# A Fourier-operator tower on one core: fused stage in a new order of units, spectra stored by group, mode and image, mix product and its copy in halves

## The chip, the cores and the metric

The kernel runs on one NeuronCore of a Trainium2 chip. The metric is the device time of one execution in microseconds. The engines are TensorE (PE, with its weight loads PEld), VectorE (DVE), ScalarE (ACT), GpSimd (POOL) and SyncE (SP, whose queue issues most DMAs). Everything is fp32.

## The reference, cut to what matters

Nearly all of the work that the change touches is the tower of four Fourier layers. 64 images of 64 by 64 pixels with 3 channels are lifted to 64 channels, and then:

```python
h = jnp.einsum('bhwi,ic->bhwc', x, fc0_w) + fc0_b          # the lift
for l in range(LAYERS):                                     # 4 layers
    xf = jnp.fft.rfft2(h)
    top = jnp.einsum('bixy,ioxy->boxy', xf[:, :, :M1, :M2], w1)     # 16 x 16 modes
    bot = jnp.einsum('bixy,ioxy->boxy', xf[:, :, -M1:, :M2], w2)
    sc = irfft2(top and bot in place, zero elsewhere)
    y = sc + einsum('bihw,oi->bohw', h, pw_w[l]) + pw_b[l]
    y = (y - mean(y)) * rsqrt(var(y) + EPS) * gamma[l] + beta[l]    # over images and pixels
    h = gelu(y)
h = gelu(h @ fc1_w + fc1_b) @ fc2_w + fc2_b
```

An attention block, two mixtures of experts and a second attention follow on the small result; the change does not touch them.

## The kernel before, in words

The program is a chain of stages. Between two stages every engine waits for all the others (`phase_end`).

1. **spectrum0** makes the spectra of the lifted input. PE transforms the 3-channel input and turns it into 64 channels in 16 rounds (`channels0`); in each round DVE and ACT copy four PSUM banks into one of three buffers `spec0`. After every fourth round SP stores a 4 MB buffer to `spec_in` in DRAM. POOL meanwhile prepares 1 MB of weights in four pieces (`gpsimd_even`), each piece loaded, computed and stored. SP's queue has `wait_ge(even_stored, 64)` and the load of those weights ahead of the four stores; round 12 waits until the first store has landed.
2. **mix** (four times, one per layer). The modes come in 8 chunks, each of 2 units (NU = 16 units). For a chunk SP loads 2 MB of spectra (`s_sb`, three buffers) and 2 MB of mode weights (`w_sb`), ACT and DVE each turn one half over to the other partitions (`rotate`), and for each unit PE runs `product` (the pointwise weights on the spectra, into four banks), ACT copies the four banks to `x2` (`copy_product`), and PE runs `spectra` (64 matmuls of 64 by 64 weights with 128 columns, one pair of weight halves per mode) into the same banks. Then ACT squares the result twice with a running sum (`square`), DVE multiplies it with `x2` twice (`cross`) and transposes it (`turn`), and SP stores it to `spec_out`. Unit n uses banks 0 to 3 or 4 to 7 by turns. In `s_sb` an element is found at (image, mode), so one mode of all images lies 64 elements apart. The sums give the mean and the variance of the next normalisation. Near the end (`ahead`) SP waits until chunk 6 has landed, then loads what the next stage starts with.
3. **fused stage** (layers 0, 1 and 2). It works on 32 pairs of images. For pair p and quarter T of its pixels: `rows_of` (half of the inverse transform, DVE turns it over), `y_of` (the other half, `spectral`, plus in layer 0 the pointwise product of the input), in layers 1 and 2 DVE adds the stored pointwise part (`add`), ACT applies Gelu in place (`gelu`), DVE transposes it (`px_turn`), PE makes the next layer's pointwise part (`next_of`), ACT copies it out (`evict`) and squares the PSUM slot with a running sum, and PE transforms the transposed pixels forward (`w_dft`, `h_dft`, DVE turning each over with `w_turn` and `h_turn` into `xs`). SP stores the pointwise part of a pair to `y_dram` (two DMAs of 1 MB) and loads the pair after next (2 MB in layers 1 and 2; 48 KB pieces of the input in layer 0), and stores four pairs' spectra at once.
4. **last stage** (layer 3's inverse, the two dense layers), then the small tail.

The fused stage's order is written out by hand: each engine has a loop over n with calls for pair n (`now`), n - 1 (`before`) and n + 1 (`after`). PSUM is cut into slots of two banks; slots 0 and 1 serve `rows_of`, `y_of` and `next_of`, banks 4 to 7 the forward transforms. A unit waits until the unit that used its slot before has been read out:

```python
ROWS_SLOT = (0, 1)
Y_SLOT = (0, 0, 1, 0)
NEXT_SLOT = (0, 1, 1, 1)
```

In layer 0 a `y` is read out by `gelu` (the semaphore `drained` is `h_made`), in layers 1 and 2 by `add` (`drained` is `y_added`). A slot of `next_of` is free when both the copy and the square have read it (`squared`).

## Time and profile before

| | before |
|---|---|
| runs (3) | 5169.06, 5176.79, 5186.94 us; median 5176.79 |
| the profiled execution | 5171.28 us, of which the span from first to last instruction 5169.4 us |
| PE, PEld busy | 3833.6 us (74%), 2200.9 us (43%) |
| DVE, ACT, POOL busy | 2339.6 us (45%), 2245.7 us (43%), 173.6 us (3%) |
| mean granted TensorE clock | 0.850 |
| moved by DMA | 800.11 MB, 155 GB/s on average |

No engine is busy all the time, and the stages have different limits, so the shares over the span say little; the stages are read one by one. The clock is a share: 1.0 is 2.4 GHz and 0.5 is 1.2 GHz, so 0.81 is a mixture in time of the two.

### The profile page before, as it was taken

The numbers are of one execution on the slowest core, as the hardware profiler recorded it, in microseconds if no ns is written. First come the engines' busy times: TensorE is split into PE (matmuls) and PEld (weight loads), VectorE is DVE, ScalarE is ACT, GpSimd is POOL, SyncE is SP. The second block draws the span as 40 slices with busy tenths as digits, with TensorE's granted clock in tenths as the row PEclk, the third lists the DMA queues.
The fourth block names the chain that finished last, engine by engine and source line by source line (L and its number), as shares of the span: only waits on it lengthen the run. The fifth ranks groups of instructions, "written<-read, shape, count | busy, mean of one in ns | idle before, by whom it ended". The sixth has DMA issues, their size and how long they took to land. (4 is left out here: it accounts for less than half of the span.)

```text
span 5169.4 us, 141776 instructions
## 1 busy us (share of the span) xinstructions
PE 3833.6 (74%) x64580; PEld 2200.9 (43%) x64580; DVE 2339.6 (45%) x2458; ACT 2245.7 (43%) x2564; POOL 173.6 (3%) x249
## 2 busy tenths in 40 slices
PE   5768878886856666765866667665769999676877
PEld 3544444444633333432643333333544444263342
DVE  2434434443445554553445555454433333355456
ACT  1434544443434444443444444443436666422222
POOL 1003100000000000000000000000000001200000
PEclk8889999997878888886878888888879999867878
DMA  6646544546556666655656656656654333101123
GB/s 232 250 138 166 142 124 124 140 123 211 193 174 184 177 172 193 182 170 183 231 159 179 189 176 175 190 165 200 238 192 155 143 145 130 36 1 43 25 65 76
DMA packets 162307, 800.11 MB, mean 155 GB/s; under 512 B 26889, under 2 KB 33361, under 8 KB 111854
## 3 DMA queue, kind: packets, MB, share of 16 engines
q1 hardware_dynamic: 150876, 776.16, 49.5%
q0 software_dynamic: 7936, 13.65, 0.8%
q8 instruction: 517, 8.47, 0.7%
q10 hardware_dynamic: 2898, 1.17, 0.1%
q14 instruction: 80, 0.66, 0.0%
HBM read 448.68 MB, written 342.23 MB: 153 GB/s over the span
## 5 line engine op out<-in xcount | busy, mean ns | idle before, releaser
L826 DVE TENSOR_TENSOR arena<-bank,arena 128x1024 f32<-128x1024 f32 x384 | 468.2, 1219 | 1047.0 <-PE bank L809 1047.0
L809 PE MATMUL bank<-fb,arena 64*64 64x128 f32 x16384 | 685.9, 304 | 299.7 <-issue 134.6
L809 PEld LDWEIGHTS bank<-fb,arena 64*64 64x64 f32 x16384 | 570.4, 197 | 639.9 <-issue 584.3
L1006 ACT ACTIVATE arena<-arena,shift,scale 128x1024 f32<-128x1024 f32 x256 | 317.7, 1241 | 862.0 <-DVE arena L826 853.7
L933 PE MATMUL bank<-arena,wst 64*64 64x512 f32 x3072 | 496.0, 687 | 146.8 <-issue 146.8
L603 PE MATMUL bank<-arena 64*64 64x128 f32 x8192 | 461.6, 393 | 132.5 <-ACT arena L631 100.0
L818 DVE STREAM_TRANSPOSE arena<-bank 128x1024 f32<-128x1024 f32 x256 | 317.6, 1241 | 518.4 <-PE bank L799 518.4
L964 PE MATMUL bank<-arena,ghq 32*32 32x256 f32 x12288 | 381.9, 501 | 190.5 <-issue 110.7
L603 PEld LDWEIGHTS bank<-arena 64*64 64x64 f32 x8192 | 408.2, 173 | 212.8 <-issue 186.8
L1013 ACT ACTIVATE arena<-bank 128x1024 f32<-128x1024 f32 x384 | 392.2, 1021 | 199.2 <-DVE arena L1046 141.8
L1046 DVE STREAM_TRANSPOSE arena<-arena 128x1024 f32<-128x1024 f32 x384 | 462.8, 1212 | 0.6 <-ACT arena L1003 0.6
L799 PE MATMUL bank<-arena,ga 64*64 64x256 f32 x4096 | 321.0, 430 | 126.6 <-DMA arena<-spec_out 54.9
L964 PEld LDWEIGHTS bank<-arena,ghq 32*32 32x32 f32 x12288 | 223.2, 119 | 403.4 <-issue 357.4
L1014 ACT ACTIVATE bank<-bank 128x1024 f32<-128x1024 f32 x384 | 391.7, 1020 | 0.0
L947 PE MATMUL bank<-arena,fwq 32*32 32x256 f32 x12288 | 321.7, 412 | 57.1 <-issue 45.7
L684 DVE SCALAR_TENSOR_TENSOR arena<-bank,arena 128x1024 f32<-128x1024 f32 x128 | 156.3, 1225 | 411.6 <-ACT arena L642 410.9
L1003 ACT ACTIVATE arena<-bank,shift,scale 128x1024 f32<-128x1024 f32 x128 | 154.2, 1205 | 410.2 <-PE bank L913 410.2
L799 PEld LDWEIGHTS bank<-arena,ga 64*64 64x64 f32 x4096 | 176.0, 147 | 354.5 <-issue 286.5
L575 PE MATMUL bank<-arena,wst 64*64 64x512 f32 x512 | 232.8, 1033 | 84.8 <-ACT arena L626 84.8
L642 ACT ACTIVATE arena<-bank 128x1024 f32<-128x1024 f32 x128 | 131.2, 1025 | 363.6 <-PE bank L603 355.7
L1176 PE MATMUL bank<-arena,fc 64*128 64x512 f32 x1024 | 274.6, 635 | 18.9 <-ACT arena L1240 18.9
L1240 ACT ACTIVATE arena<-bank,fc1b 128x1024 f32<-128x1024 f32 x256 | 272.2, 1100 | 19.6 <-PE bank L1176 19.5
(240 smaller groups left out, 3961.5 us busy)
## 6 DMA issues: line engine op xcount, KB each, us to landing
y_dram<-arena SPq DMA_DIRECT2D x192, 1024.0 KB, 10.3
arena<-y_dram SPq DMA_DIRECT2D x96, 2048.0 KB
arena<-spec_in SPq DMA_DIRECT2D x32, 2048.0 KB, 7.9
spec_out<-arena SPq DMA_DIRECT2D x128, 512.0 KB, 8.7
arena<-in_w_modes SPq DMA_DIRECT2D x28, 2048.0 KB, 13.8
arena<-spec_out SPq DMA_DIRECT2D x112, 512.0 KB, 11.7
spec_in<-arena SPq DMA_DIRECT2D x24, 2048.0 KB, 7.6
spec_in<-arena SPq DMA_DIRECT2D x4, 4096.0 KB, 24.8
```

The costliest lines, as they stand in the source:

```text
L603: mm = pe.matmul(bank[4 * v + q][ROW[h], k * 2 * B:(k + 1) * 2 * B], w_sb[c % 3][ROW[row], mode, :], z[ROW[row], :, :, mode], start=(swap ...
L799: mm = pe.matmul(bank[2 * s + v][CHAN[par], :].rearrange("p (c r k) -> p r k c", c=16, r=2)[:, r], ga[k_p, r * S:(r + 1) * S], grp[p // Q ...
L809: mm = pe.matmul(hpx(bank[2 * s + i][CHAN[v], :])[:, :, j * S:(j + 1) * S], a2[p % 2][CHAN[i], :, v, 4 * T + j], hpx(fb2[CHAN[i], :]), sta ...
L818: dve.transpose(a2[p % 2].rearrange("p (v c) a m -> p v (c a m)", v=2)[:, :, hc * 512:(hc + 1) * 512], slot(s)).then_inc(rows_turned, 1)
L826: dve.tensor_tensor(chunk(p, T), slot(s), chunk(p, T), ALU.add).then_inc(y_added, 1)
L933: mm = pe.matmul(bank[2 * NEXT_SLOT[T] + v][CHAN[i], :], wst[CHAN[v], :], pb[p % NS][CHAN[v], i, T * BK:(T + 1) * BK], start=True, stop=Tr ...
L947: mm = pe.matmul(bank[4 + g][QUAD[c], 0:256], fwq[QUAD[g], s * 32:(s + 1) * 32], hT[p % 2][QUAD[g], i, :, s, c * CQ:(c + 1) * CQ], start=( ...
L964: mm = pe.matmul(bank[4 + c][QUAD[j], 256:512], ghq[QUAD[c], col:col + K1], t1[p % 2][QUAD[c], hh * 2 + v, :, :, ri * M2:(ri + 1) * M2], s ...
L1006: act.activation(chunk(p, T), chunk(p, T), ACT.Gelu, bias=shift[:], scale=scale[:]).then_inc(h_made, 1)
L1013: act.activation(chunk(p, T), slot(NEXT_SLOT[T]), ACT.Copy).then_inc(evicted, 1)
L1014: act.activation(slot(NEXT_SLOT[T]), slot(NEXT_SLOT[T]), ACT.Square, accum_out=acc[:, p * 4 + T:p * 4 + T + 1]).then_inc(squared, 1)
L1046: dve.transpose(hT[p % 2].rearrange("p i h s c -> p i (h s c)")[:, :, T * BK:(T + 1) * BK], chunk(p, T)).then_inc(px_turned, 1)
```

## The change

**spectrum0.** The stores of the four buffers no longer stand behind `even_stored`; the wait and the load of the even weights come after them. `spec_in` and `spec0` are laid out by (group of 8 images, mode, image of the group), and each copy of two banks is cut into two of one bank.

**mix.** `s_sb` and `r_sb` have the new layout, so that 8 images of a mode lie side by side and 4 modes of a group are 32 elements side by side. `product` is now 16 matmuls of 256 columns (before: 4 of 512 and 8 of 256), and it and its copy are in two halves, each with its own count: PE starts `spectra` on the first two banks when their copy is done. On ACT the order is square of the first half, both copies of the next unit, square of the second half; on DVE the cross of the second half comes first, before any square. `turn` waits for both squares.

**Fused stage.** A new order of the units on PE, ACT and DVE; `y_of(p, 1)` moves to slot 1; `h_dft` comes a pair later; `gelu` of quarter 3 moves behind the next pair's first units on ACT; the square reads what `evict` has written in SBUF (into a scratch buffer at the arena's end) and stands apart from it, so that a slot is free after the copy; SP's reload of a pair's buffer also waits for its squares.

**Elsewhere.** Some small tensors move into the arena, which grows by 1024 elements; scratch places shift; two more waits for `zeroed`. The last stage and the tail are as before.

The core of the diff:

```diff
 # spectrum0, SP's queue
-            sp.wait_ge(even_stored, 64)
-            load_even(sp, 0)
             for t in range(NB):
                 sp.wait_ge(fc0_first, 4 * t + 4)
                 sp.wait_ge(fc0_second, 4 * t + 4)
...
+                sp.dma_start(spec_in[:, :, gs].rearrange("h p g x -> p h (g x)"), spec0[t % 3]).then_inc(spec0_stored[min(t, 1)], 16)
+            sp.wait_ge(even_stored, 64)
+            load_even(sp, 0)
 # mix
-        s_sb = [at(S_AT + u * B * MC, B, MC) for u in range(3)]
+        s_sb = [at(S_AT + u * B * MC, NG, MC * GI) for u in range(3)]
...
-                        if q % 2 == 0:
-                            mm = pe.matmul(bank[4 * v + q][ROW[h], :], wst[ROW[0], :],
-                                           z[ROW[0], :, :, m0:m0 + 4].rearrange("p r b m -> p m r b"),
-                                           start=True, stop=True, tile_position=(0, h * C))
...
+                        for r in range(2):
+                            part = z[ROW[0], r] if q % 2 == 0 else z[ROW[1], 1 - r]
+                            w = wst[ROW[0], :] if q % 2 == 0 else (wst, wneg)[r][ROW[1], :]
+                            mm = pe.matmul(o[:, r], w, part[:, :, m0:m0 + 4, :].rearrange("p g m b -> p g (m b)"),
+                                           start=True, stop=True, tile_position=(q % 2 * C, h * C))
+                    if q % 2 == 1:
+                        mm.then_inc(prod_done, 1)
...
-                pe.wait_ge(prod_copied, l * NU + n + 1)
...
+                    if swap == 0:
+                        pe.wait_ge(prod_copied, (l * NU + n) * 2 + pair + 1)
...
-                                               w_sb[c % 3][ROW[row], mode, :], z[ROW[row], :, :, mode],
+                                               w_sb[c % 3][ROW[row], mode, :], z[ROW[row], :, :, mode, :],
 # fused stage
-        Y_SLOT = (0, 0, 1, 0)
+        Y_SLOT = (0, 1, 1, 0)
...
-            for n in range(NP + 1):
-                now, before, after = n < NP, n > 0, n + 1 < NP
+            for n in range(NP + 2):
+                now, before, after = n < NP, 0 < n <= NP, n + 1 < NP
                 if now:
                     y_of(n, 0)
-                if before:
-                    next_of(n - 1, 2)
-                if now:
                     y_of(n, 1)
+                if n > 1:
+                    h_dft(n - 2)
                 if before:
                     next_of(n - 1, 3)
...
-                act.activation(slot(NEXT_SLOT[T]), slot(NEXT_SLOT[T]), ACT.Square, accum_out=acc[:, p * 4 + T:p * 4 + T + 1]).then_inc(squared, 1)
+
+            def square(p, T):
...
+                act.activation(junk_p.rearrange("p (i x) -> p i x", i=2), chunk(p, T), ACT.Square,
+                               accum_out=acc[:, p * 4 + T:p * 4 + T + 1]).then_inc(squared, 1)
```

How the new order stands on the engines is best read from the programs' own rows. First PE in the fused stage of layers 1 and 2, from one `y_of(n, 0)` on. L809 is `y_of` (16 matmuls), L933 `next_of`, L799 `rows_of`, L947 `w_dft`, L964 `h_dft`; the ISA and REGISTER_ALU rows compute semaphore values. Before:

```order
L809 MATMUL bank<-fb,arena 64x2x64 x16
L922 REGISTER_ALU
L933 MATMUL bank<-arena,wst 64x512 x4
L903 REGISTER_ALU
L809 MATMUL bank<-fb,arena 64x2x64 x16
L922 REGISTER_ALU
L933 MATMUL bank<-arena,wst 64x512 x4
L890 ISA
L799 MATMUL bank<-arena,ga 64x16x16 x8
L947 MATMUL bank<-arena,fwq 32x256 x32
L809 MATMUL bank<-fb,arena 64x2x64 x16
```

The same place of the change, where L822 is `y_of`, L954 `next_of`, L812 `rows_of`, L970 `w_dft` and L985 `h_dft`:

```order
L822 MATMUL bank<-fb,arena 64x2x64 x32
L985 MATMUL bank<-arena,ghq 32x256 x64
L938 REGISTER_ALU
L948 REGISTER_ALU
L954 MATMUL bank<-arena,wst 64x512 x4
L903 ISA
L812 MATMUL bank<-arena,ga 64x16x16 x8
L822 MATMUL bank<-fb,arena 64x2x64 x16
L970 MATMUL bank<-arena,fwq 32x256 x32
```

The first two `y_of` now stand together, `h_dft` of an older pair fills the place after them, and one `next_of` has moved to the end of the turn.

ACT at the same stage. Before, L1006 is `gelu`, L1013 the copy and L1014 the square, always in this order:

```order
L1006 ACTIVATE arena<-arena,shift,scale 128x2x512
L1013 ACTIVATE arena<-bank 128x2x512
L1014 ACTIVATE bank,acc<-bank 128x1024
L1005 ISA
L1006 ACTIVATE arena<-arena,shift,scale 128x2x512
L1013 ACTIVATE arena<-bank 128x2x512
L1014 ACTIVATE bank,acc<-bank 128x1024
```

In the change L1027 is `gelu`, L1034 the copy and L1041 the square, which now reads the arena:

```order
L1034 ACTIVATE arena<-bank 128x2x512 x2
L1026 REGISTER_ALU
L1027 ACTIVATE arena<-arena,shift,scale 128x2x512
L1041 ACTIVATE arena,acc<-arena 128x1024
L1026 ISA
L1027 ACTIVATE arena<-arena,shift,scale 128x2x512
L1041 ACTIVATE arena,acc<-arena 128x1024
```

Two copies come first in a turn, and a square never stands between a copy and the next unit's use of its slot.

ACT in the mix, from the first copy of a product on. Before, L631 is the copy, L642 the square, L626 the turning over:

```order
L631 ACTIVATE arena<-bank 128x2048
L626 ACTIVATE arena<-arena 64x4096
L642 ACTIVATE arena,acc<-bank 128x1024 x2
L631 ACTIVATE arena<-bank 128x2048
L642 ACTIVATE arena,acc<-bank 128x1024 x2
```

In the change L634 is the copy, L646 the square, L628 the turning over:

```order
L646 ACTIVATE arena,acc<-bank 128x1024
L634 ACTIVATE arena<-bank 128x1024 x2
L646 ACTIVATE arena,acc<-bank 128x1024
L628 ACTIVATE arena<-arena 64x4096
L646 ACTIVATE arena,acc<-bank 128x1024
```

The copies of the next unit's two halves now stand between the two squares of this unit.

## Rows read from the trace of the kernel before

**Rows 1.** Windows: length, PE, PEld, DVE, ACT, POOL busy, clock, DMA share, GB/s

```profile
0.00:124.00 124.00, 68.61 (x460) 50.34 (x460) 34.03 (x42) 17.58 (x17) 25.30 (x37) 0.82 0.63 230
...
357.00:1217.00 860.00, 684.66 (x15360) 368.38 (x15360) 346.36 (x320) 405.31 (x513) 71.42 (x73) 0.93 0.53 139
1217.00:1451.00 234.00, 171.73 (x2434) 126.98 (x2434) 96.50 (x117) 97.46 (x92) 0.00 (x0) 0.81 0.62 216
1451.00:2431.00 980.00, 652.18 (x14336) 369.08 (x14336) 488.25 (x448) 422.48 (x513) 0.37 (x1) 0.81 0.59 174
...
2666.00:3622.00 956.00, 646.38 (x14336) 366.33 (x14336) 488.46 (x448) 422.50 (x513) 0.37 (x1) 0.82 0.62 180
```

**Rows 2.** Timeline of spectrum0, DVE and SP: start, us, what, idle before

```profile
93.26 2.35 DVE L341 COPY arena<-bank 128x1024 f32<-128x1024 f32 x2 [30.99 <-DMA spec_in<-arena]
...
77.25 22.74 SPq L245 DMA_DIRECT2D spec_in<-arena  x4
```

**Rows 3.** Timeline of PE, two units of the mix of layer 1

```profile
1286.24 7.21 PE L603 MATMUL bank<-arena 64*64 64x128 f32 x128 [2.06 <-ACT arena L631]
...
1299.00 7.17 PE L603 MATMUL bank<-arena 64*64 64x128 f32 x128 [2.09 <-ACT arena L631]
```

**Rows 4.** PE lines one by one: duration ns min/median/max

```profile
L575 PE MATMUL bank<-arena,wst x512: 1030/1032/1113, 135.9 to 3820.3; 64*64 64x512 f32 x171
...
L913 PE MATMUL bank<-arena,wx x1024: 586/589/1112, 367.3 to 1180.5; 64*64 64x512 f32 x171
...
L603 PE MATMUL bank<-arena x8192: 377/392/473, 141.6 to 3830.3; 64*64 64x128 f32 x200
...
L809 PE MATMUL bank<-fb,arena x16384: 266/275/479, 366.3 to 4473.6; 64*64 64x128 f32 x200
...
L799 PE MATMUL bank<-arena,ga x4096: 372/376/687, 361.2 to 4452.4; 64*64 64x256 f32 x196
```

**Rows 5.** Timeline of SP, end of the mix of layer 1

```profile
1414.85 4.88 SPq L523 DMA_DIRECT2D spec_out<-arena  x4
...
1451.88 0.82 SPq L769 DMA_DIRECT2D arena<-spec_out  x2
```

**Rows 6.** Timeline of PE, one pair of the fused stage of layer 1

```profile
2010.91 1.19 PE L809 MATMUL bank<-fb,arena 64*64 64x128 f32 x32
...
2013.55 1.19 PE L809 MATMUL bank<-fb,arena 64*64 64x128 f32 x32 [0.59 <-DVE arena L826]
2016.85 1.34 PE L933 MATMUL bank<-arena,wst 64*64 64x512 f32 x8 [2.11 <-issue]
...
2024.32 1.09 PE L799 MATMUL bank<-arena,ga 64*64 64x256 f32 x16 [0.57 <-DVE arena L826]
...
2028.80 1.19 PE L809 MATMUL bank<-fb,arena 64*64 64x128 f32 x32 [1.84 <-ACT bank L1014]
...
2032.57 1.32 PE L964 MATMUL bank<-arena,ghq 32*32 32x256 f32 x45 [1.72 <-DVE arena L1053]
2035.36 3.34 PE L964 MATMUL bank<-arena,ghq 32*32 32x256 f32 x83 [1.47 <-issue]
2038.62 1.99 PE L809 MATMUL bank<-fb,arena 64*64 64x128 f32 x32
```

**Rows 7.** Groups of instructions by shape, ACT and PE: busy us, mean ns, idle before

```profile
L1006 ACT ACTIVATE arena<-arena,shift,scale 128x1024 f32<-128x1024 f32 x256 | 317.7, 1241 | 862.0 <-DVE arena L826 853.7
...
L1013 ACT ACTIVATE arena<-bank 128x1024 f32<-128x1024 f32 x384 | 392.2, 1021 | 199.2 <-DVE arena L1046 141.8
...
L913 PE MATMUL bank<-arena,wx 64*64 64x512 f32 x1024 | 152.0, 638 | 5.6 <-issue 5.6
```

**Rows 8.** Timeline of PE in layer 0's fused stage

```profile
780.80 1.19 PE L809 MATMUL bank<-fb,arena 64*64 64x128 f32 x32 [0.56 <-ACT arena L1003]
...
790.27 1.09 PE L799 MATMUL bank<-arena,ga 64*64 64x256 f32 x16 [0.53 <-ACT arena L1003]
```

**Rows 9.** Timeline of PE in layer 1's fused stage, a gap inside one unit

```profile
2064.30 1.33 PE L809 MATMUL bank<-fb,arena 64*64 64x128 f32 x18 [6.45 <-issue]
```

More of the change, by code:

```diff
@@ new lines, in square @@
+            def square(n, h):
+                if h == 0:
+                    act.wait_ge(mix_done, l * NU + n + 1)
+                else:
+                    act.wait_ge(crossed, (l * NU + n) * 2 + 1)
+                act.sem_inc(waited[act.engine], 1)
+                if n == 0 and h == 0:
+                    act.activation(junk_dc[C:P], bank[0][C:P, 0:2 * B], ACT.Square, accum_out=acc[C:P, ACC - 1:ACC])
+                act.wait_ge(s_squared, (l * NU + n) * 2 + h)
+                act.sem_inc(waited[act.engine], 1)
+                act.activation(junk, quarter(n % 2, h), ACT.Square, accum_out=acc[:, P + 2 * n + h:P + 2 * n + h + 1]).then_inc(s_squared, 1)
@@ L645, in scalar_mix @@
             rotate(0)
-            copy_product(0)
+            for h in range(2):
+                copy_product(0, h)
             for n in range(NU):
-                square(n)
+                square(n, 0)
                 if n + 1 < NU:
-                    copy_product(n + 1)
+                    for h in range(2):
+                        copy_product(n + 1, h)
+                square(n, 1)
                 if n % 2 == 0 and n // 2 + 1 < NCH:
@@ L982, in tensor_fuse @@
                     rows_of(n + 1, 0)
+                if now:
+                    y_of(n, 2)
                 if before:
@@ L995, in tensor_fuse @@
                 if before:
-                    h_dft(n - 1)
+                    w_dft(n - 1, 1)
+                if now:
+                    next_of(n, 2)
         def scalar_fuse(act, l, first):
@@ L1019, in scalar_fuse @@
                     evict(n - 1, 1)
+                    evict(n - 1, 2)
+                    gelu(n - 1, 3)
+                    square(n - 1, 0)
                 if now:
@@ L1027, in scalar_fuse @@
                     evict(n - 1, 3)
+                    square(n - 1, 2)
                 if now:
@@ L1030, in scalar_fuse @@
                     evict(n, 0)
-                    gelu(n, 3)
+                if before:
+                    square(n - 1, 3)
         def vector_fuse(dve, l, first):
```

197 lines of the change are left out of this document (99 added, 98 removed).

## The prediction

> **What bounds the kernel now.** I read the windows by stage first [rows 1]. The reader is to see two kinds of stage. In a mix (234 us, four times) PE is busy for 172 us, ACT and DVE for 97 each. In a fused stage of layers 1 and 2 (980 and 956 us) PE is busy for 650 us at a clock of 0.81, DVE for 488, ACT for 422; in layer 0's (860 us) PE for 685 us at 0.93. None is bound by one engine's work: PE waits for slots. The DMA share gives a floor: 0.62 x 234 = 145 us in a mix, 0.59 x 980 = 578 us in a fused stage, 18.1 us for each of its 32 pairs. Then the timelines. In the mix a unit takes 12.76 us (1286.24 to 1299.00), of which 7.2 are `spectra`, 2.07 a wait for the copy, and the rest, 3.5, `product` [rows 3]. In a fused pair of 27.7 us, PE waits five times for a slot or an operand, 0.59 + 2.11 + 0.57 + 1.84 + 1.72 = 6.8 us [rows 6]. "Issue" at 2016.85 is such a wait: `next_of` 3 waits for the square of quarter 2.
>
> **spectrum0.** DVE and ACT stand 31 us until the first store has landed, and that store is issued only at 77.25, when POOL has stored its last piece of weights [rows 2]. In the new order the first store goes out after round 3, near 40 us, and takes some 12 us (four took 77.25 to 124, the end of the stage). So the 31 us go. What is late next: the engines' chain after round 12 ended 24 us after 93.26, so now near 86; the last store goes out at about 69 and lands at about 82; POOL's three remaining pieces, each a load and a store, now share the DMA engines with 4 MB stores. I estimate 20 us more for them (bounds 10 and 30), which gives an end at 97 in place of 124: **-27 us** (-17 to -37). The copies in two halves cost PSUM reads of half length; they lie beside PE and I take them at nothing. If strided writes took twice as long, 16 rounds would cost some 1.2 us each, 19 us, still within the range.
>
> **Mix.** Two edits count. First, the stride. L575 and L913 both run 64 by 64 weights with 512 columns, and take 1032 and 589 ns; the one reads elements 64 apart, the other neighbours. L603 and L809 both have 128 columns, and take 392 and 275 [rows 4]. From 256 and 128 columns (minima 372 and 266) a column costs 0.83 ns and the fixed part is 160 ns. Without it the ratios are 872/429 = 2.03 and 232/106 = 2.2: a matmul that reads with this stride runs at half rate. In the new layout `product` reads 32 neighbours and `spectra` 8; the arrangement of `spectra`'s instructions is that of L809, 32 instructions in 1.19 us with a flight of 0.27 [rows 6], so 30 ns each and 128 x 0.030 + 0.2 = 4.0 us. `product` takes half of 3.5, 1.8. Second, the halves: the copy of a half takes 1.02 us (the time of an equal copy, L1013 [rows 7]), the first half's while PE makes the second, so that nearly all of the 2.07 us goes. PE's unit would be 5.8 us; but ACT has 97.5/16 = 6.1 us of work per unit, DVE 6.0, and the DMA floor is 145/16 = 9.1 with the loads of the stage's edges and some 7.8 without (about 20 us of edges). I take 8.5 us, between these. What is late next is the spectra and weights of the next chunk, and `turn`, which waits for the second square. The 37 us from chunk 6's store to the end (1414.85 to 1451.88 [rows 5]) are DMA and stay. So 14 units x 4.26 = 60, and 3 at the start (a shorter first product and copy): -63 per mix, **-252 us** for four. Bounds: 7.8 us per unit gives -72 per mix; only the copy hidden, 10.8 us, gives -29.
>
> A word on the other side of `product`: it now writes PSUM in runs of 8 elements. L799 (`rows_of`) writes with a step of 32 elements, and takes 376 ns for 256 columns, the price of its columns and no more [rows 4]. So I charge nothing. The Trainium skill (Advanced Engine Details and Errata, PSUM Cachelines) says that any non-contiguous PSUM pattern slows matmuls significantly; the trace does not agree for L799. By that rule `product` would keep its 3.5 us, which is a rival below.
>
> **Fused stage, layers 1 and 2.** I laid one pair out on PE, DVE and ACT, each operation with the duration of its row (DVE's at the mean of 488.25/448 = 1.1 us [rows 1], `gelu` 1.24, copy 1.02, square 1.24 because it now reads SBUF as L1006 does [rows 7], plus its sum of 0.2), each starting when its engine and its semaphores allow. The waits for squares go, and `h_dft` no longer waits for the `w_turn` just before it. Left are waits for copies: 0.4 us before `y_of` 1, 2.2 before `y_of` 2 (the copy of quarter 3 stands behind a gelu and a square on ACT), 0.7 before `y_of` 3, 3.3 in all. ACT works 4 x (1.24 + 1.02 + 1.44) = 14.8 us per pair, below any period in question. So 6.8 - 3.3 = 3.5 us per pair, 112 us per stage. The clock adds to it: the same 14336 instructions keep PE busy for 684.7 - 152.0 (L913, which only layer 0 has [rows 7]) = 533 us at 0.93 and 652 at 0.81 [rows 1], so 119 us lie between. Denser work should recover some of it; I take three eighths, 45 us (bounds 0 and 119). Against it stand gaps in the middle of a unit that no semaphore explains: 1.47 us in `h_dft` [rows 6], 6.45 in a `y_of` [rows 9]. They come while the pair's store is under way, and with a DMA share of 0.69 instead of 0.59 fewer of them fall into waits: +16. Sum -141 per stage, **-282 us**. Both stages then stand near 840 and 815 us, above the DMA floor of 578.
>
> The Trainium skill (Runtime: NRT & Kernel Launch, Instruction fetch mechanics) has instruction fetch mostly hidden; if these gaps are something else than fetch, the 16 us per stage may be absent. No row says which they are.
>
> **Fused stage, layer 0.** Here `gelu` reads the slot itself. The waits are 0.56 us before `y_of` 1 and about 0.53 before each `rows_of`, 1.6 us per pair [rows 8]. In the new order `y_of(n, 0)` waits for `gelu(n - 1, 3)`, which stands behind the copies of quarters 1 and 2, the second of a unit that PE has only just ended: 2.7 us, and two waits of 0.4 for copies, 3.5 in all. That is 1.9 us more per pair, 61 per stage; but longer waits also cover gaps such as those above, at which I take back 1.3 us per pair: **+20 us** (0 to +60).
>
> Last stage and tail: no change. A DVE write in steps of 8 elements (`h_turn`, two half-length ones per pair) is not in the trace; below, nothing; above, a DVE operation more per pair, 1.1 us [rows 1], beside a DVE that is idle for half of the stage. I take nothing.
>
> **Sum.** -27 - 252 - 282 + 20 = -541. The profiled execution took 5171, so 4630; the median of the runs shown stands 5 above it: **4635 us**.
>
> **Rivals.**
> 1. *The stride isn't it* (the slow columns come from the order of quadrants, say). For: L575 stands among other shapes. Against: two pairs of lines with ratios of 2. Then only the copy is hidden, -29 per mix: 4635 + 4 x 34 = 4771. Chance 0.08.
> 2. *PSUM writes*: `product` stays at 3.5 us, a unit at about 9.7: 14 x 1.2 x 4 = 67 more, 4702. Against: L799. Chance 0.05.
> 3. *DMA and the gaps bound the fused stage*. A pair's store and load fill 18.1 us; if the gaps grow with it, 2 us per pair of the gain in layers 1 and 2 and 1 us in layer 0 are lost: 4 x 32 + 32 = 160 more, 4795. For: rows 9. Chance 0.13.
> 4. *Better*: the clock comes back wholly (-74 per stage of layers 1 and 2), the mix reaches 7.8 (-36 in all), layer 0 costs nothing: 4635 - 148 - 36 - 20 = 4431. Chance 0.14.
> 5. *Slower than before*: slot 1 becomes a chain. It serves six units of a pair (`rows_of` 1, `y_of` 1 and 2, `next_of` 1 to 3), slot 0 four; a use is a fill of 1.2 us and a read of 1.2, with handovers 2.6, so six make 16 us. To eat the 279 us of mix and spectrum0 the three stages (96 pairs) would each have to lose 2.9 us per pair, to over 32 us, so 5.4 us per use, twice as long as it is. Time then over 5190. Chance 0.02.
>
> **Numbers.** The forecast itself (both gains, within +-80 us) has 0.58. The range must reach towards rivals 2, 3 and 4: 4480 to 4810. A difference under 0.3% (16 us) can't be told from none. Faster 0.97, same 0.01, slower 0.02.
>
> **What would show it.** spectrum0: the first mix load near 97 us and no wait of 31 us. Mix: `spectra`'s matmuls at 275 ns instead of 392, a unit of 8 to 9 us, PE waiting for `turn` or for loads. Fused stage: no wait for a square, PE's waits for copies at 3 to 4 us per pair, a clock above 0.85 in layers 1 and 2, about 26 us per pair; in layer 0 a wait of 2 to 3 us before `y_of(n, 0)`. Wrong would be: units of 10.8 us (rival 1), a DMA share near 0.8 with a pair at 28 us (rival 3), or matmuls that wait for slot 1 throughout.

## The result and the profile after

| | before | after |
|---|---|---|
| runs | 5169.06 to 5186.94 us, median 5179.23 (4 runs) | 4740.92 to 4763.59 us, median 4753.9 (4 runs) |
| ratio | | 0.9178, 95% interval 0.9147 to 0.9209 |
| span of the profiled execution | 5169.4 us | 4744.5 us |
| granted TensorE clock | 0.850 | 0.868 |

The forecast was 4635 us (4480 to 4810): faster, as it came, but by 425 us in place of 541. First the windows by stage, as in [rows 1], with the same columns (length, PE, PEld, DVE, ACT, POOL busy, clock, DMA share, GB/s). The borders are the first loads of a mix and the first `rows_of` of a fused stage.

```profile
0.00:99.00 99.00, 67.77 (x460) 49.25 (x460) 45.80 (x58) 33.20 (x33) 25.29 (x37) 0.95 0.78 279
287.00:1168.00 881.00, 695.99 (x15360) 381.56 (x15360) 373.24 (x320) 412.44 (x512) 69.85 (x70) 0.89 0.52 135
1168.00:1366.00 198.00, 112.22 (x2562) 94.82 (x2562) 96.90 (x117) 98.04 (x109) 0.37 (x1) 0.80 0.77 258
1366.00:2211.00 845.00, 612.27 (x14336) 358.48 (x14336) 514.53 (x448) 414.41 (x512) 0.00 (x0) 0.86 0.68 201
2410.00:3240.00 830.00, 602.29 (x14336) 352.87 (x14336) 514.50 (x448) 414.33 (x512) 0.00 (x0) 0.88 0.70 204
```

With the borders taken the same way in both traces, the stages account for the whole difference:

| us | before | after | difference | forecast |
|---|---|---|---|---|
| spectrum0 | 124.2 | 99.2 | -25.0 | -27 |
| four mixes | 237.0, 237.9, 238.6, 237.1 | 188.1, 198.3, 199.0, 189.4 | -175.7 | -252 |
| fused stage, layer 0 | 856.2 | 880.6 | +24.4 | +20 |
| fused stages, layers 1 and 2 | 975.7, 945.2 | 845.1, 830.0 | -130.5, -115.2 | -141 each |
| last stage and tail | 1317.5 | 1314.6 | -2.9 | 0 |

**spectrum0.** SP's timeline, which answers to [rows 2], has the four stores from 40.25 on and the mix's first loads at 99.24. What ends last now is POOL's last piece of weights: SP waits until 97.62 for its store, then loads the even weights.

```profile
40.25 37.66 SPq L244 DMA_DIRECT2D spec_in<-arena  x4
97.62 0.35 SPq L511 DMA_DIRECT2D arena<-w_even  x1
99.24 0.81 SPq L519 DMA_DIRECT2D arena<-spec_in  x2
```

**Mix.** The two matmul lines one by one (duration ns min/median/max), as in [rows 4]. `spectra` is L605, before 377/392; `product` is L583, now with 256 columns.

```profile
L605 PE MATMUL bank<-arena x8192: 266/269/473, 115.6 to 3402.0; 64*64 64x128 f32 x200
L583 PE MATMUL bank<-arena,wneg x512: 373/376/631, 113.2 to 3391.7; 64*64 64x256 f32 x171
```

L605 has just the price of L809 with as many columns [rows 4]. The waits of PE in the mix of layer 1, 1195 to 1325 us (total, times, longest), show what is left:

```profile
PE bank L605 <- issue: 20.6, 10, 3.9
PE bank L583 <- DVE arena L671: 10.1, 4, 3.2
PE bank L605 <- ACT arena L634: 3.9, 9, 0.6
```

The wait for the copy has shrunk from 2.07 us per unit to 0.6 at most. New are a wait of the next chunk's product for DVE's `rotate` (L671), and gaps inside `spectra` that no semaphore explains. Now the end of that mix on SP, as in [rows 5]: L528 stores a chunk, L782 and L792 load for the next stage.

```profile
1325.42 4.89 SPq L528 DMA_DIRECT2D spec_out<-arena  x4
1337.57 0.38 SPq L782 DMA_DIRECT2D arena<-spec_out  x1
1338.01 1.89 SPq L792 DMA_DIRECT2D arena<-y_dram  x2
1340.10 1.84 SPq L528 DMA_DIRECT2D spec_out<-arena  x4
...
1362.83 0.82 SPq L782 DMA_DIRECT2D arena<-spec_out  x2
```

From chunk 6's store to the row at 1362.83, where all stores have landed, pass 37.4 us, as before (37.0). But the last store is issued 2 us after 4 MB of pair loads and takes 22.7 us to land. In the kernel before the same row stood almost 14 us behind the loads, and the store landed in 11.6 us (to 1451.88 [rows 5]):

```profile
1440.25 4.83 SPq L523 DMA_DIRECT2D spec_out<-arena  x4
```

**Fused stage, layer 1.** The last two thirds of one pair on PE, which answers to [rows 6] (L985 `h_dft`, L954 `next_of`, L812 `rows_of`, L822 `y_of`, L970 `w_dft`):

```profile
1815.93 0.34 PE L822 MATMUL bank<-fb,arena 64*64 64x128 f32 x1 [0.42 <-ACT arena L1034]
1821.20 1.98 PE L822 MATMUL bank<-fb,arena 64*64 64x128 f32 x31 [4.92 <-issue]
1823.12 3.04 PE L985 MATMUL bank<-arena,ghq 32*32 32x256 f32 x97
1828.16 0.72 PE L985 MATMUL bank<-arena,ghq 32*32 32x256 f32 x31 [2.01 <-issue]
1828.81 1.84 PE L954 MATMUL bank<-arena,wst 64*64 64x512 f32 x8
1830.41 1.95 PE L812 MATMUL bank<-arena,ga 64*64 64x256 f32 x16
1832.11 1.23 PE L822 MATMUL bank<-fb,arena 64*64 64x128 f32 x32
```

The reader is to see that the semaphore wait is 0.42 us, and that the time goes at 1821.20 and 1828.16, in the middle of a unit: 1 of 32 matmuls had run, then nothing for 4.92 us. All PE waits of 1500 to 2150 us (24.6 pairs):

```profile
PE bank L822 <- issue: 68.2, 22, 5.9
PE bank L970 <- issue: 41.6, 15, 6.7
PE bank L822 <- ACT arena L1034: 23.2, 52, 0.7
PE bank L985 <- issue: 21.8, 14, 4.9
PE bank L812 <- issue: 7.7, 4, 2.5
PE bank L954 <- issue: 6.8, 2, 3.6
PE bank L954 <- DVE arena L831: 1.1, 3, 0.5
```

The same view of the kernel before, 1600 to 2350 us (24.5 pairs):

```profile
PE bank L933 <- issue: 56.0, 29, 2.3
PE bank L809 <- issue: 37.4, 13, 6.4
PE bank L809 <- ACT bank L1014: 36.5, 21, 1.8
PE bank L964 <- issue: 32.7, 15, 4.7
PE bank L964 <- DVE arena L1053: 30.1, 24, 1.7
PE bank L947 <- issue: 15.1, 7, 3.8
PE bank L799 <- DVE arena L826: 13.8, 24, 0.6
PE bank L809 <- DVE arena L826: 12.4, 22, 0.6
```

The row of L933 is the wait for the square (about once per pair, 1.9 us), whatever its releaser says. So waits for semaphores fell from 148.8/24.5 = 6.1 us per pair to 24.3/24.6 = 1.0, and gaps rose from 85.2/24.5 = 3.5 to 146.1/24.6 = 5.9.

What the gaps wait for can be read from the packets of the traces, which list the 16 KB packets of the instruction queue beside the data. Before the two gaps shown, such a packet passed from 1818.90 to 1819.77 and from 1825.67 to 1826.55: PE went on 1.4 and 1.6 us after its end. Over layer 1's fused stage PE stops 56 times for more than 1 us without a semaphore to name, 169 us in all. 54 of these stops, 165 us, end 1.2 to 1.6 us after the end of an instruction packet; of the 72 waits for a semaphore 8 do, and of moments drawn at random 8%. In the kernel before, without the waits for the square at L933, it is 35 of 36 stops, 102 of 104 us. So, as nearly as a trace can show it, in these gaps PE waits for its own instructions. A packet takes as long in both (median 0.96 us): it isn't slower, it comes late.

**Fused stage, layer 0.** The wait before `y_of(n, 0)` is there, 2.4 us once a pair, forecast at 2.7 us:

```profile
796.60 1.19 PE L822 MATMUL bank<-fb,arena 64*64 64x128 f32 x32 [2.37 <-issue]
```

In the middle of the stage the waits for `gelu` and copies come to 3.41 us per pair (before 1.66), and the gaps fell from 3.26 to 1.81. PE's clock fell from 0.93 to 0.89, and its busy time rose from 684.7 to 696.0 us.

### The profile page after: what moved, and what is told of

The parts are those of the page before. It is cut to its first block and busy times, and to the rows that moved or that the text cites. A ratio compares the mean times of both kernels' runs of the same rounds, so it can differ in the third digit from the quotient of the medians.

```text
span 4744.5 us, 143699 instructions
## 1 busy us (share of the span) xinstructions
PE 3513.1 (74%) x65092; PEld 2052.3 (43%) x65092; DVE 2431.2 (51%) x2474; ACT 2252.6 (47%) x2644; POOL 173.3 (4%) x249
## 3 DMA queue, kind: packets, MB, share of 16 engines
q8 instruction: 521, 8.54, 0.7%
## 5 line engine op out<-in xcount | busy, mean ns | idle before, releaser
L822 PE MATMUL bank<-fb,arena 64*64 64x128 f32 x16384 | 699.0, 310 | 342.7 <-issue 236.1
L822 PEld LDWEIGHTS bank<-fb,arena 64*64 64x64 f32 x16384 | 613.2, 199 | 640.0 <-issue 584.3
L1034 ACT ACTIVATE arena<-bank 128x1024 f32<-128x1024 f32 x384 | 393.0, 1023 | 888.9 <-PE bank L954 546.3
L954 PE MATMUL bank<-arena,wst 64*64 64x512 f32 x3072 | 471.8, 672 | 36.3 <-issue 27.2
L831 DVE STREAM_TRANSPOSE arena<-bank 128x1024 f32<-128x1024 f32 x256 | 317.2, 1239 | 271.3 <-PE bank L812 271.3
L970 PE MATMUL bank<-arena,fwq 32*32 32x256 f32 x12288 | 329.6, 403 | 145.7 <-issue 141.4
L1027 ACT ACTIVATE arena<-arena,shift,scale 128x1024 f32<-128x1024 f32 x256 | 316.3, 1235 | 240.5 <-DVE arena L839 240.5
L1086 DVE STREAM_TRANSPOSE arena<-bank 128x1024 f32<-128x1024 f32 x192 | 237.6, 1237 | 375.5 <-PE bank L970 375.5
L1041 ACT ACTIVATE arena<-arena 128x1024 f32<-128x1024 f32 x384 | 402.4, 1048 | 0.7
L985 PE MATMUL bank<-arena,ghq 32*32 32x256 f32 x12288 | 330.8, 443 | 71.3 <-issue 66.1
L812 PE MATMUL bank<-arena,ga 64*64 64x256 f32 x4096 | 294.3, 397 | 118.2 <-DMA arena<-spec_out 95.2
L605 PE MATMUL bank<-arena 64*64 64x128 f32 x8192 | 278.4, 285 | 90.3 <-issue 69.4
L605 PEld LDWEIGHTS bank<-arena 64*64 64x64 f32 x8192 | 252.6, 141 | 127.2 <-issue 125.6
L970 PEld LDWEIGHTS bank<-arena,fwq 32*32 32x32 f32 x12288 | 162.5, 105 | 331.2 <-issue 286.4
L812 PEld LDWEIGHTS bank<-arena,ga 64*64 64x64 f32 x4096 | 162.0, 139 | 313.5 <-issue 236.9
L1095 DVE STREAM_TRANSPOSE arena<-bank 128x512 f32<-128x512 f32 x192 | 196.2, 1098 | 197.0 <-PE bank L985 197.0
L985 PEld LDWEIGHTS bank<-arena,ghq 32*32 32x32 f32 x12288 | 197.3, 111 | 207.2 <-issue 161.2
L583 PE MATMUL bank<-arena,wst 64*64 64x256 f32 x1536 | 170.5, 477 | 154.4 <-ACT arena L628 86.6
```

The lines of the kernel that those rows point to most:

```text
L605: mm = pe.matmul(bank[4 * v + q][ROW[h], k * 2 * B:(k + 1) * 2 * B], w_sb[c % 3][ROW[row], mode, :], z[ROW[row], :, :, mode, :], start=(sw ...
L812: mm = pe.matmul(bank[2 * s + v][CHAN[par], :].rearrange("p (c r k) -> p r k c", c=16, r=2)[:, r], ga[k_p, r * S:(r + 1) * S], grp[p // Q ...
L822: mm = pe.matmul(hpx(bank[2 * s + i][CHAN[v], :])[:, :, j * S:(j + 1) * S], a2[p % 2][CHAN[i], :, v, 4 * T + j], hpx(fb2[CHAN[i], :]), sta ...
L831: dve.transpose(a2[p % 2].rearrange("p (v c) a m -> p v (c a m)", v=2)[:, :, hc * 512:(hc + 1) * 512], slot(s)).then_inc(rows_turned, 1)
L954: mm = pe.matmul(bank[2 * NEXT_SLOT[T] + v][CHAN[i], :], wst[CHAN[v], :], pb[p % NS][CHAN[v], i, T * BK:(T + 1) * BK], start=True, stop=Tr ...
L970: mm = pe.matmul(bank[4 + g][QUAD[c], 0:256], fwq[QUAD[g], s * 32:(s + 1) * 32], hT[p % 2][QUAD[g], i, :, s, c * CQ:(c + 1) * CQ], start=( ...
```

## The experiments

Each was run beside the kernel before; ratios are to it (the change: 0.9178). Stages are read as in the table above.

**1. Only the lift's stores not held back, on the kernel before.**

```diff
-            sp.wait_ge(even_stored, 64)
-            load_even(sp, 0)
             for t in range(NB):
...
+            sp.wait_ge(even_stored, 64)
+            load_even(sp, 0)
             sp.wait_ge(spec0_stored[1], 16 * (NB - 1))
```

> The kernel before with one edit: the four lift stores go out ahead of the wait for the even weights. Theory A, the 31 us wait came from the queue order alone and the copies in halves and the new layout cost nothing there: the first loads of the mix go out at 99 us (124 before, 99.2 in the changed kernel), all later stages stay, the time falls by 25 us to about 5154. Rival B, the new layout of the copies is part of the gain or hides a loss: the first loads at 92 or less, or at 105 or more.

Measured: spectrum0 97.9 us in place of 124.2; 5163.8 us, ratio 0.9952 (0.9925 to 0.9978), 21 us less than the kernel before beside it. The whole gain of the stage is the queue's order (A). This run also shows how much the fused stages vary from one execution to the next with nothing changed in them: 863, 963 and 966 us where the kernel before had 856, 976 and 945.

**2. The mix with a whole product and copy and the old orders on ACT and DVE; the layout as changed.**

```diff
-                    if q % 2 == 1:
-                        mm.then_inc(prod_done, 1)
+                mm.then_inc(prod_done, 1)
...
-                        pe.wait_ge(prod_copied, (l * NU + n) * 2 + pair + 1)
+                        pe.wait_ge(prod_copied, l * NU + n + 1)
```

> The changed kernel with the product counted and copied whole and ACT and DVE in their old order in the mix; layout, matmul shapes, lift and fused stage as changed. Changed kernel: mixes of 188 to 199 us, before 237. Theory A, the reads at half rate were most of what the change took away and the halves hide one copy per unit: a mix of 205 to 220 us, time 4754 + 60 to 100. Theory B, the mix is now bound by its DMA traffic, so that the halves bring nothing: mixes within 4 us of the changed kernel's, time within 15 us. Theory C, the halves are most of it: mixes of 225 us or more.

Measured: mixes of 199, 207, 210 and 209 us; 4808.6 us, ratio 0.9269 (0.9243 to 0.9294). PE's timeline shows the wait for the copy in its old size:

```profile
1281.98 5.39 PE L604 MATMUL bank<-arena 64*64 64x128 f32 x128 [2.08 <-ACT arena L632]
```

So the layout alone is worth 38, 31, 29 and 28 us, the halves the other 11, 9, 11 and 19. That is A, with the layout worth more than its numbers (205 to 220 us for a mix leave 17 to 32 for it), and layer 0's mix below them. B falls, since the halves do bring something although the DMA share is already 0.77.

**3. The old order, slots and square in the fused stage; lift and mix as changed.**

```diff
-        Y_SLOT = (0, 1, 1, 0)
+        Y_SLOT = (0, 0, 1, 0)
...
-            for n in range(NP + 2):
-                now, before, after = n < NP, 0 < n <= NP, n + 1 < NP
+            for n in range(NP + 1):
+                now, before, after = n < NP, n > 0, n + 1 < NP
```

> The changed kernel with PE's, ACT's and DVE's order, slots and square of the fused stage as before; lift and mix as changed. Theory A, the fused stages' times follow from the order alone: 856, 976 and 945 us again (changed: 881, 845, 830), time 4754 + 222 = 4976. Rival B, part of it comes from elsewhere (the layout in which h_turn writes, the state in which the stage starts): stages that stand over 15 us from these. Mixes stay at 188 to 199 us in both.

Measured: 862.8, 976.9 and 984.0 us; 5016.7 us, ratio 0.9686 (0.9653 to 0.9719). Layers 0 and 1 are A's to within 7 us; layer 2 is 39 above it, more than the 21 us that experiment 1 showed as a stage's own variation and by B's condition a case for B; no run tells which. So a difference of one layer 2 stage is uncertain by some 20 to 40 us. Either way the order carries the fused stages' gain: back in its old form, layers 1 and 2 lose 132 and 154 us.

**4. A sixteenth of each pair's store.**

```diff
-  y_dram[p]...[i], pb[p % NS][CHAN[i]]
+  y_dram[p]...[i, :, :, 0:128], pb[p % NS][CHAN[i], :, 0:128]
```

> The changed kernel, but of each pair's pointwise part only a sixteenth is stored to DRAM, and the loads of 2 MB per pair take the same bytes from the mode weights instead (so the result is not the reference's). In the changed kernel PE loses about 5.9 us per pair of layers 1 and 2 to gaps in the middle of units that no semaphore explains, before 3.5. Theory A, these gaps come while the stores occupy the DMA engines: the gaps fall below 2 us per pair and stages 1 and 2 from 845 and 830 us to about 700 to 730. Rival B, the gaps belong to PE's instruction stream whatever the DMA engines do: gaps of 5 to 6 us per pair, stages above 810. In between: the loads do it as well.

Measured, in one run: 4333.6 us; fused stages of 790, 670 and 666 us. Layer 1's window, and PE's waits of 1400 to 1850 us (21.5 pairs):

```profile
1282.00:1952.00 670.00, 548.19 (x14336) 330.38 (x14336) 511.79 (x448) 413.44 (x512) 0.00 (x0) 0.95 0.44 159
```

```profile
PE bank L822 <- ACT arena L1034: 24.6, 54, 0.8
PE bank L822 <- issue: 16.2, 10, 2.5
PE bank L970 <- issue: 15.1, 9, 2.6
PE bank L985 <- issue: 7.9, 13, 1.3
```

A holds, with stages shorter than it said (700 to 730): the gaps fall from 5.9 to 2.0 us per pair, and with them goes the low clock, 0.86 to 0.95, so that the same 14336 instructions keep PE busy for 548 us in place of 612. Together these would be 125 + 64 = 189 us; the stage lost 175. The stores cost a fifth of the stage, and no wait of any engine named them. The stops that are left are of the same kind, 25 of 27 over 1 us. The kernel computes with other data here, and no run tells whether that bears on the clock.

**5. The pair stored in one DMA of 128 partitions, the reordering done by the load.**

```diff
-  for i in range(2): y_dram[p]("(v c) (i x) -> i c v x")[i] <- pb[CHAN[i]]
+  y_dram[p]("p (v x) -> p v x") <- pb
-  pb <- y_dram[p]("p (i x) -> p i x")
+  for v in range(2): pb[CHAN[v]] <- y_dram[p]("(i c) (v x) -> v c i x")[v]
```

> The changed kernel with a pair's pointwise part stored in one DMA of 128 partitions and 16 KB packets (changed: two of 64 partitions and 8 KB packets, which take 10 us for 2 MB) and with the reordering done by the load, in two DMAs of 64 partitions (changed: one of 128). Shrinking the stores took 175 us off stage 1, by gaps inside units and by the clock. Theory A, what disturbs PE is how long the DMA engines are busy with a pair, and the store is slow by its shape: the store takes 6 us, stage 1 falls by 60 us or more. Rival B, writes to DRAM are slow whatever their shape: the store takes 9 to 10 us still, the load gets slower by its 8 KB packets, and stage 1 stays within 25 us of 845 or gets longer.

Measured: 4758.5 us, ratio 0.9182 (0.9134 to 0.923); fused stages 820, 858 and 863. The page's DMA issues (count, KB each, median us from issue to landing), first of the change, then of this kernel:

```profile
y_dram<-arena SPq DMA_DIRECT2D x192, 1024.0 KB, 11.1
```

```profile
y_dram<-arena SPq DMA_DIRECT2D x96, 2048.0 KB, 8.5
```

Neither theory is right. The store did get faster, so writes are not slow as such. But the load now moves 8 KB packets to 64 partitions and became as slow as the store had been: by the packets of the trace one of 8 KB took 576 ns on average in the changed kernel's store and 595 in this kernel's load, one of 16 KB 711 and 707 in layer 1. What a pair wins in the store it loses in the load. In layer 0, which has no such load, the stage got 61 us shorter. PE's stops over 1 us in layer 1 add up to 179 us (169 in the changed kernel), and all 51 end behind an instruction packet.

**6. Stores in halves, spread over the turn.**

```diff
+                if 0 < n <= NP:
+                    store(n - 1, 0)
                 if n < NP:
                     load_piece(sp, l, n)
...
-                    store(n - 1)
+                    store(n - 1, 1)
```

> The changed kernel with the store of a pair in two times two DMAs: quarters 0 and 1 as soon as they are copied out, quarters 2 and 3 as now. The same bytes, in packets of 4 KB, spread over the turn. Theory A, PE's gaps come because a burst of some 17 us holds back the fetch of PE's instructions: with two shorter bursts the gaps of 5.9 us per pair fall to 4 or less, stages 1 and 2 by 40 us or more. Rival B, only the amount of traffic counts: stages within 20 us of 845 and 830. Rival C, the smaller packets cost more than the spreading gives: stages longer by 20 us or more.

Measured: 4509.8 us, ratio 0.8711 (0.8659 to 0.8763); fused stages 817, 751 and 743. Gaps of 3.9 us per pair, clock 0.91 and 0.92. A's numbers; experiment 9 shows that its reason, the spreading, was wrong.

**7. `rotate` a unit earlier on ACT and DVE.**

```diff
-                if n % 2 == 0 and n // 2 + 1 < NCH:
-                    rotate(n // 2 + 1)
+                if n == 0:
+                    rotate(1)
+                if n % 2 == 1 and (n + 3) // 2 < NCH:
+                    rotate((n + 3) // 2)
```

> The changed kernel with the turning over of a chunk's spectra (rotate) on ACT and DVE one unit earlier, at the end of the odd unit in place of the end of the even one. Now a chunk of the mix takes 20.9 us, and PE waits 2.1 to 2.5 us per chunk for DVE's rotate, which stands behind the turn, which stands behind ACT's second square. Theory A, that chain of engines holds the mix at 10.4 us per unit where I forecast 8.5: mixes fall by 12 us or more each, time by 50. Rival B, the DMA engines hold it (6 MB per chunk at a share near 1): the wait moves from rotate's place to the loads, mixes stay within 5 us or get longer, time within 20 us.

Measured: 4726.4 us, ratio 0.9127 (0.9058 to 0.9196), mixes 187.5, 194.8, 191.0 and 186.4: 0.6 to 8.0 us less each, 15 in all. That lies between the theories, three of the four mixes within B's 5 us: the chain through `turn` holds the mix a little. B's reason does not fit either, since the DMA share from 1220 to 1320 us of the changed kernel is 0.81 and not near 1. What is left of the gain stands in the fused stages (6 to 9 us less each), which the edit doesn't touch and which vary by more than that.

**8. The pair loads behind the mix's last store.**

```diff
             load_group(sp, l, 0, slice(NCH - 1, NCH))
+            if not first:
+                for p in range(2):
+                    load_pair(sp, l, p)
```

(and none in `ahead`; the last stage likewise.)

> The changed kernel with the loads of the first two pairs (4 MB) issued behind the store of the last chunk of a mix and behind the last piece of the spectra, not ahead of them. From PE's last matmul of a mix to the first of the next stage pass 34.9 and 34.1 us in layers 1 and 2 and 26.7 and 27.8 in 0 and 3; before the change 21.6 to 21.9. Theory A, the mix is now so fast that its last store queues behind those 4 MB, which takes back some 13 us of its gain in layers 1 and 2: the tails fall to 22 to 26 us, the first pair starts some 2 us later, time falls by 15 to 25 us. Rival B, the tail is the drain of the chunk stores before it: tails within 4 us of now.

Measured: 4721.3 us, ratio 0.9103 (0.9052 to 0.9154); from PE's last `spectra` to the next stage 20.8, 24.4, 24.1 and 20.6 us in place of 26.7, 34.9, 34.1 and 27.8. The last store of layer 1's mix lands in 14.0 us where it took 22.7:

```profile
1343.87 2.22 SPq L528 DMA_DIRECT2D spec_out<-arena  x4
...
1357.83 0.35 SPq L780 DMA_DIRECT2D arena<-spec_out  x1
```

A, by its numbers, for the tails of layers 1 and 2. Less of it reaches the mixes: they last 191.1, 189.2, 187.8 and 189.7 us, 9 and 11 less in layers 1 and 2, and nothing less in 0 and 3. In those two PE's part of the mix took 8 to 9 us longer, about as much as the tail got shorter. And layer 0's program is untouched by the edit (experiment 10 has this edit too, and its tail there is 26.8 us), so that its 20.8 is no effect of the loads.

**9. The same four stores, not spread.**

```diff
+                    store(n - 1, 0)
                     store(n - 1, 1)
```

(both waiting for all four copies)

> The changed kernel with the same four DMAs of 4 KB packets per pair as in the run with halves (stages 1 and 2: 751 and 743 us, changed kernel 845 and 830), but all four issued together where the store stands now, so nothing is spread. Theory A, the spreading over the turn gave the 90 us: stages within 25 us of 845 and 830. Rival B, the size of the packets gave it (an 8 KB store packet takes 575 ns, a 4 KB one 242, and what fetches PE's instructions waits behind packets): stages within 25 us of 751 and 743. In between: both.

Measured: 4526.7 us, ratio 0.8734 (0.8686 to 0.8782); fused stages 817, 764 and 754. B: the form of the DMAs gave 81 and 76 of the 94 and 87 us, the spreading 13 at most, within what a stage varies. By the packets one of 4 KB took 240 ns on average, so a store of 512 occupies each of the 16 engines for 7.7 us where 256 of 576 ns took 9.2. PE's stops over 1 us in layer 1 fell with it, from 169 to 109 us, and 44 of the 46 end behind an instruction packet. The size of the packets and the number of DMAs changed together; no run separates them.

**10. The edits of experiments 6, 7 and 8, and pair loads in 4 KB packets too** (`y_dram` laid out by quarters of a row).

```diff
+  pb[p % NS]("p (i h x) -> p (i h) x") <- y_dram[p]("q p x -> p q x")
```

> The changed kernel with the three edits that gained, stores in halves (-244 us alone), rotate a unit early (-27) and the pair loads behind the last store of a mix (-33), and one new: the loads of a pair have 4 KB packets too (now 16 KB, 717 ns each). If the three add up, 4754 - 244 - 27 - 33 = 4450 without the new one. Theory A, large packets of loads hold back PE's instructions as those of stores do: stages 1 and 2 fall from 751 and 743 to 720 or less, time to 4400 or less. Rival B, only stores disturb: stages within 15 us of 751 and 743, time 4435 to 4465. Rival C, more packets cost DMA time: stages over 765.

Measured: 4478.0 us, ratio 0.8622 (0.8559 to 0.8684); mixes 183.7, 182.2, 184.4 and 181.4, fused stages 799, 757 and 765. B, towards C: packets of 4 KB in place of 16 in the loads bring nothing. The four mixes take 732 us together, where experiments 7 and 8 alone had 760 and 758 and the change 775.

**11. As 10, but with store packets of 2 KB, loads in 16 KB, and the old order in layer 0 alone.**

```diff
+            if first:
+                return tensor_fuse0(pe, l, first)
...
+                    for x in (xs_h.start, xs_h.start + BK):
+                        ... [i, :, :, x:x + BK] <- pb[p % NS][CHAN[i], :, x:x + BK]
```

> The changed kernel with rotate a unit early, the pair loads behind the last store of a mix, the pair's stores in halves and in DMAs with packets of 2 KB (eight per pair), loads in 16 KB packets as in the changed kernel, and the old order, slots and square in the fused stage of layer 0 alone. Store packets of 4 KB gave stages 1 and 2 of 751 and 743 us, of 8 KB 845 and 830, almost no stores 670 and 666. Theory A, the smaller the packets the less PE is disturbed: stages 1 and 2 at 735 or less. Rival B, 4 KB is small enough and more DMAs cost as much as they give: 740 to 770. Layer 0: with 8 KB packets the new order took 881 and the old 863 or 856; with 4 KB the new one 799 to 817. Theory A, the old order saves its 18 to 24 us here too: 775 to 795. Rival B, without the disturbance the new order is no worse: 795 to 820. Time by the two A: about 4440; by the two B about 4475.

Measured: 4365.1 us, ratio 0.8427 (0.8396 to 0.8457), the fastest of all kernels: 8% less than the change itself. Windows of the three fused stages:

```profile
283.00:1023.00 740.00, 643.92 (x15360) 354.34 (x15360) 369.39 (x320) 403.22 (x512) 69.82 (x70) 0.97 0.58 161
1206.00:1947.00 741.00, 579.77 (x14336) 342.60 (x14336) 514.63 (x448) 413.68 (x512) 0.00 (x0) 0.91 0.73 235
2131.00:2868.00 737.00, 575.18 (x14336) 339.73 (x14336) 514.12 (x448) 412.80 (x512) 0.00 (x0) 0.92 0.73 235
```

Layers 1 and 2 are at B's edge: 2 KB is worth 6 to 10 us over the 4 KB of experiment 6, no more than a stage varies. Layer 0 falls to 740 us, 77 below experiment 6 and beyond A. It has two edits, the old order and the packets; experiment 12 has the old order with 4 KB packets and takes 778 us there, so that about 40 of the 77 are the order's. What gave the other 38 no run shows alone.

**12. The kernel before with 4 KB store packets.**

```diff
+                for xs_h in (slice(0, 2 * BK), slice(2 * BK, 4 * BK)):
                     for i in range(2):
```

> The kernel before with one edit: a pair's stores in four DMAs of 4 KB packets, all issued where they stand now. In the changed kernel this took 81 and 76 us off stages 1 and 2. The order of the fused stage was worth 131 and 115 us there with 8 KB packets. Theory A, in the kernel before part of the disturbance fell into waits for slots that were there anyway, so that less is won: stages 1 and 2 from 976 and 945 to 910 to 940 and 880 to 910, time 5050 to 5090. That would mean that the order alone is worth more, some 160 us a stage, once the packets are small. Rival B, the two are independent: 895 and 869 or less, time below 5020. Rival C, the disturbance was hidden: stages within 20 us of now.

Measured: 4987.2 us, ratio 0.9612 (0.9589 to 0.9635), with fused stages of 778, 905 and 911. The time is B's, but only because layer 0, which neither theory had, got 79 us shorter; layers 1 and 2, by 70 and 34, are at the edges of A. Against experiment 9, the same store in the new order, the order costs 40 us in layer 0 and gains 141 and 158 in the others; with 8 KB packets it cost 24 and gained 131 and 115. That is what A said: the order is worth more once the packets are small.

## Why the prediction was right, and where it was short

The time came out 119 us above the forecast: inside the range, but outside the +-80 us that had 0.58, and by the number alone nearer to rival 1 (4771) and rival 3 (4795). The direction, the two gains and the edits that carry them are as forecast (experiments 1 to 3); the sizes were not all.

**spectrum0, -27: right**, term by term: the first store at 40.25, the last at 68.6 (forecast 40 and 69), the end at 99.2 (97). Experiment 1 has it alone.

**Mix, -252: the mechanism right, the size 76 us too large.** The stride was what I took it for: 269 ns in place of 392, with the price of neighbouring elements (rival 1 is out). Writes to PSUM in runs of 8 elements cost `product` nothing: 376 ns for 256 columns, L799's 376 [rows 4]; rival 2, and by the rows the rule of the Trainium skill (Advanced Engine Details and Errata, PSUM Cachelines), does not hold here. The halves hid the copy: 2.07 us down to 0.6 at most. The term that was mis-sized is "I take 8.5 us" for a unit. From the first product to the last `spectra` pass 148.5 to 152.1 us, 9.4 per unit; before 203.7 to 204.1. That is 53 us less, where 16 units of 4.26 and the 3 at the start would be 71: 18 us a mix, 72 of the 76. What stands there in place of the 0.9 us: gaps inside `spectra` (20.6 us in 130, some 1.5 per unit) and the wait for `rotate`, of which experiment 7 got back 15 us over the four mixes. The gaps are those of the fused stage: all 7 over 1 us in the mix of layer 1 end behind an instruction packet, and the mix before has none. The sum had no term for them. Whether the DMA share of 0.77 holds the mix too no run tested.

"The 37 us [...] are DMA and stay" held in layer 1, 37.4. The last chunk's two units lie inside them, which is why the sum has 14 units; it so allowed for a tail longer by 8.5 us behind PE's last `spectra`, and the tails are longer by 5 to 13, 36 over four mixes. In layers 1 and 2 the last store ran into the pair loads, as experiment 8 shows; moving the loads was worth 9 and 11 us there.

**Fused stage, layers 1 and 2, -141 each: right in sum (-131, -115), its terms off in both directions.** Waits were to fall by 3.5 us per pair, and fell by 5.1 (6.1 to 1.0), 163 us in layer 1. The laid-out wait of 2.2 us before `y_of` 2 was not there. That isn't because gaps on PE give ACT the time: in experiment 4 it was 0.45 us (at 1631.93) in a pair in which PE has no gap, so the layout by hand had ACT too late. The clock's term was right: PE busy fell by 40 and 44 us, forecast 45. The step that failed is "+16" for the gaps: they rose by 2.4 us per pair, 77 per stage. So -163 - 40 + 77 = -126 in layer 1. Rival 3 had named this with a price of 2 us per pair; it did not come true as a whole only because the waits fell further. Experiments 4, 5, 6 and 9 show what drives the gaps, which I had only suspected: the pair's DMA traffic, above all in DMAs with 8 KB packets. "They come while the pair's store is under way" was misread too: by the packets the gap of 1.47 us [rows 6] and nearly all of the 6.45 us [rows 9] fall where the store's packets had ended and the pair's load was under way.

**Layer 0, +20: right (+24), and in the main for the reason given.** The wait before `y_of(n, 0)` was 2.4 us (forecast 2.7), the waits together 3.41 per pair (3.5), and the gaps fell by 1.45 (1.3). That makes (1.75 - 1.45) x 32, some 10 us; another 11 are PE's busy time at the lower clock, for which the sum had no term, so that the close agreement is in part luck. That longer waits cover gaps is borne out from the other side: with less disturbance the same order costs 40 us.

**Last stage, 0:** -3. Adding up: 2 + 76 + 36 + 4 - 3 = 115 of the 116 us that were missing. The 36 are both fused stages, of which layer 2's 26 lie within what that stage varies.

**The low clock** went along with the gaps; that it is a consequence and not a price of its own is argued, not shown. In layer 1 it was 0.86 with 5.9 us of gaps per pair, 0.90 with 3.9 (experiment 9), 0.95 with 2.0 (experiment 4).

**What stays open:** what makes the instruction packets late. The page lists 521 of them with 8.54 MB, 16 KB each, one per 250 instructions of PE and its weight loads, and that PE waits for them is shown above. The Trainium skill (Runtime: NRT & Kernel Launch, Instruction fetch mechanics) has such a fetch mostly hidden; 2 to 6 us of gaps per pair were not hidden here. They grow with the bulk traffic (experiments 4 and 9), but whether a fetch queues behind data packets no row shows: of the 116 in layer 1's fused stage 23 began while packets of 8 KB filled 14 or more of the 16 engines, which they did for 34% of the time. Open is also why packets of 8 KB over 64 partitions are slow: experiment 5 excludes the direction, experiments 9 and 11 that the count of partitions alone does it.

## What to carry to other kernels

When waits for semaphores are taken out of a loop, count first the gaps that no semaphore explains: they don't go with the waits, they come out from under them, and here they took back half of what the waits gave. If the trace has instruction packets, hold the ends of the gaps against them. Look at the form of bulk DMAs even where nothing waits for them: cutting the same 2 MB store into DMAs with smaller packets was worth more (-227 us) than the whole mix edit. And where a stretch is counted as fixed, leave the work inside it out of the gain, as the 14 units of 16 did here, and ask what the faster engine will now queue behind.

## What the runs showed of the hardware

- A matmul with 128 columns took 392 ns with its moving operand 64 elements apart, and 269 with runs of 8. This agrees with the Trainium skill (Advanced Engine Details and Errata, SBUF Cachelines), which has accesses that share no 16-byte line at a penalty.
- The form of a DMA decides its rate, in both directions: over 64 partitions, packets of 8 KB took 576 to 595 ns (14 KB per us and engine), of 4 KB 240 (17); over 128 partitions, 16 KB took 707 to 711 (23). The times are means from the packets of the traces in layer 1's fused stage.
- PE ran out of instructions in the middle of a unit: 54 of its 56 stops over 1 us in layer 1's fused stage (165 of 169 us) ended 1.2 to 1.6 us after a 16 KB packet of the instruction queue.
- An activation with Square took 1048 ns from SBUF, with 192 for reading its sum, where I had taken 1240: from PSUM it took 1018. Nor is the longer time of L1006 [rows 7] that of reading SBUF, since the same Gelu took 1204 from PSUM (L1003); what is Gelu's and what its operands `scale` and `shift` cost, no run separates.
- Bulk stores that nobody waits for took 175 us of an 845 us stage, some two thirds by stopping PE between two matmuls and one third by the lower clock that goes with it (125 and 64 us by the rows of experiment 4, one run, which sum to 189).
